# A rebuilt prologue in an attention and mixture-of-experts block: routing keys on TensorE, first row maxima beside the low halves

## The reference

```python
xn = layernorm(x)                                # x: 32 x 256 tokens x 128, eps 1e-5
q = xn @ Wq.T                                    # 8 heads of 32
kv = xn @ Wkv_down.T                             # rank 64
k, v = kv @ Wk_up.T, kv @ Wv_up.T
attn = softmax(q @ k.T * 32 ** -0.5)             # per batch of 256 tokens and head
a = (attn @ v) @ Wo.T
keys = xn @ wr + br
expert = mod(floor(keys), 8)
for e in range(8):                               # each token keeps its own expert's y
    y = relu(xn @ W1[e] + b1[e]) @ W2[e] + b2[e] # 128 -> 512 -> 128
out = x + a + y
```

## Time and profile before

| | |
|---|---|
| median of three runs | 561.96 us |
| the profiled execution | 561.93 us, of which the span shown is 560.1 us |
| busy share of the span | TensorE 83%, VectorE 84%, ScalarE 68%, GpSimd 70% |
| prologue (to the first exponential) | about 101 us |
| a unit in the first half | about 10.4 us |

### The profile page before, as it was taken

One profiled execution on the slowest core, in us unless ns is written; L12 is line 12 of the kernel. 1 busy time (PEld: TensorE's weight loads), 2 busy tenths in 40 slices (PEclk: granted clock), 3 DMA queues, 4 the chain that ended last, 5 costly groups with the idle time before them and its releaser, 6 DMA issues.

```text
span 560.1 us, 15849 instructions
## 1 busy us (share of the span) xinstructions
PE 462.7 (83%) x5016; PEld 299.0 (53%) x5016; DVE 471.7 (84%) x1000; ACT 382.0 (68%) x957; POOL 392.3 (70%) x362
## 2 busy tenths in 40 slices
PE   0433444999999999998699999998989999999984
PEld 0222211545455455455499999996545545645532
DVE  4897749799999999989688888887698988988985
ACT  0767931576777777777577777775677867877784
POOL 4166740689889888944377777775977977978970
PEclk9999757899999999999999999999999999999998
DMA  7995363455456456444778888881544764755531
GB/s 187 291 380 200 143 156 76 91 131 122 109 120 133 108 116 134 106 86 103 232 215 272 266 260 265 272 254 50 133 100 104 146 127 112 146 120 117 106 82 49
DMA packets 84956, 87.08 MB, mean 155 GB/s; under 512 B 10433, under 2 KB 66337, under 8 KB 84897
## 3 DMA queue, kind: packets, MB, share of 16 engines
q1 hardware_dynamic: 80800, 77.92, 53.1%
q0 software_dynamic: 4096, 8.40, 6.6%
HBM read 38.94 MB, written 22.04 MB: 109 GB/s over the span
## 4 chain that ended last, share of the span: by engine, by line
PE 38%; DVE 18%; issue 17%; POOL 14%; DMA 4%; SPq 4%; ACT 3%; DVEq 1%; POOLq 1%; ACTq 0%
POOL split L444 12%; PE psum L1061 8%; PE psum L1091 8%; DVE negm L858 6%; PE psum L1075 6%; PE psum L1106 4%; PE psum L1012 3%; PE psum L1124 3%; PE psum L1013 3%; PE psum L1014 3%; DVE oTl L872 2%; DMA stk<-mT 2%; DVE split L757 2%; DVE acc L877 2%; SPq L286 1%
## 5 line engine op out<-in xcount | busy, mean ns | idle before, releaser
L598 ACT ACTIVATE prob<-psum 128x512 f32<-128x512 f32 x256 | 151.1, 593 | 94.4 <-PE psum L1075 93.3
L858 DVE TENSOR_REDUCE negm<-psum 128x2 f16<-128x512 f32 x256 | 172.8, 683 | 36.6 <-PE psum L1061 35.3
L490 POOL TENSOR_TENSOR padd<-prob 128x512 f32<-128x512 f32 x120 | 139.2, 1160 | 44.9 <-ACT prob L598 42.8
L1061 PE MATMUL psum<-stk 96*128 96x256 f16 x512 | 100.7, 279 | 12.4 <-DVE negm L858 11.3
L444 POOL TENSOR_TENSOR split<-xTl,split 128x512 f16<-128x512 f32 x72 | 83.3, 1157 | 33.1 <-DVE split L948 33.1
L667 ACT ACTIVATE xTl<-psum,xn_all 128x128 f32<-128x128 f32 x288 | 82.0, 368 | 28.2 <-POOL split L444 23.4
L1075 PE MATMUL psum<-stk 97*128 97x256 f16 x512 | 98.0, 273 | 3.3 <-DMA stk<-mT 2.9
L460 POOL DMA_INDIRECT xsort<-xn_all,pos x64 | 63.0, 984 | 31.2 <-DVE pos L840 19.1
L1061 PEld LDWEIGHTS psum<-stk 96*128 96x128 f16 x512 | 38.2, 99 | 72.0 <-DVE negm L858 33.4
L468 POOL DMA_INDIRECT xn_all<-ysort,pos x64 | 64.1, 1001 | 12.1 <-issue 8.9
L1091 PE MATMUL psum<-prob,vt 128*32 128x256 f32 x1024 | 68.5, 385 | 0.7 <-ACT prob L598 0.7
(11 more groups left out here) (143 smaller groups left out, 984.7 us busy)
## 6 DMA issues: line engine op xcount, KB each, us to landing
stk<-split SPq DMA_DIRECT2D x192, 128.0 KB
xn_all<-wsplit SPq DMA_DIRECT2D x72, 258.0 KB, 4.3
xsort<-prob SPq DMA_DIRECT2D x9, 512.0 KB, 6.4
xTh<-xsort SPq DMA_DIRECT2D x18, 256.0 KB, 3.9
ysort<-xTh SPq DMA_DIRECT2D x18, 256.0 KB, 4.1
stk<-W SPq DMA_DIRECT2D x16, 256.0 KB, 5.5
wsplit<-stk SPq DMA_DIRECT2D x16, 256.0 KB, 3.8
out<-acc SPq DMA_DIRECT2D x16, 256.0 KB
```

The lines of the kernel that those rows point to most:

```text
L490: nc.gpsimd.tensor_tensor(padd[:, bb, hs], prob[:, bb, hs, 0, :], prob[:, bb, hs, 1, :], ALU.add).then_inc(pool_add, 1)
L598: nc.scalar.activation(prob[:, bb, h, :, :].rearrange("p a c -> p (a c)"), bank[2 + n % 2], ACT.Exp, scale=SCALE).then_inc(act_exp, 1)
L858: V.tensor_reduce(negm[:, k % 2, col:col + 2], bank[n % 2].rearrange("p (a c) -> p a c", a=2), AX.X, ALU.max, negate=True).then_inc(dve_ma ...
L1061: ins = mm(bank[n % 2][:, qc * T:(qc + 1) * T], stk[0:96, s, 1, h, t0 + qc * P:t0 + (qc + 1) * P], stk[0:96, s, 0, h, t0:t0 + T], start=Tr ...
```

## The change

Tokens are laid out in `acc` in another order inside a batch: partition p holds tokens 2p and 2p + 1, for the loads of x and for the stores of the output. The first quarter of x comes in four transfers, each with its own semaphore, and the other three quarters behind the small weights. ScalarE no longer waits for the small weights ahead of the first square root.

The prologue's loop is one step after the other on all engines. ScalarE normalises two chunks of a step and GpSimd the other two. TensorE makes the routing keys from `xTh` and `xTl` against `wr` in three float16 parts (eight small products for a step, `token_keys`). The projections for units 0 to 2, the values of unit 0, and unit 0's scores and row maxima lie between the steps. An expert's weights are split after the steps of the table `WSTEP` = (4, 6, 8, 9, 11, 12, 14, 15). The ranks are cut in four parts, made by VectorE in rounds 0, 2, 4 and 6 of unit 0. The eight stores of zeros, now from one row of zeros, are issued in units 0 and 1, around the loads for later units. The scatters run in units 2 to 14, and the loads of the experts' second matrices (`load_w2`) are shifted by that. Statistics, constants and staging have other homes in SBUF.

The cut diff:

```diff
+            for s in range(4):
+                sp.dma_start(acc_of(4 * s, 4), rows_of(x_rows, 4 * s, 4)).then_inc(sp_x0[s], 16)
...
+            for q in range(1, 4):
+                sp.dma_start(acc_of(q * NC // 4, NC // 4), rows_of(x_rows, q * NC // 4, NC // 4)).then_inc(sp_x[q], 16)
+
+            def load_weights(e):
+                sp.dma_start(wstage[e % 4][:, 0:F], W1[e]).then_inc(sp_w[e % 4], 16)
+                sp.dma_start(wstage[e % 4][:, F:2 * F].rearrange("p (c d) -> p c d", c=FC),
+                             W2[e].rearrange("(c p) d -> p c d", p=P)).then_inc(sp_w[e % 4], 16)
 
             def store_weights(e):
+                sp.wait_ge(pool_lo, e + 1)
...
+                    zeros = half == 0 and first and k < 2
+                    if zeros:
+                        store_zeros(4 * k)
+                        store_zeros(4 * k + 1)
                     if not (last and k >= 1):
                         load_stack(u + 3, k + 3)
+                    if zeros:
+                        store_zeros(4 * k + 2)
                     if not (last and k == 3):
                         load_max(u + 1, k + 1)
+                    if zeros:
+                        store_zeros(4 * k + 3)
                     if stores:
...
+                load_w2(E - 2, 0, NIT // 2)
                 load_w2(E - 1, 1, NIT // 2)
...
+            for e in range(4):
+                load_weights(e)
+            load_stack(0, 0)
+            load_stack(1, 1)
+            sp.wait_ge(act_cast, 3)
+            sp.dma_start(wsplit[:, :, F:W1E // 2].rearrange("e p c -> p e c"),
+                         b1c[:].rearrange("p (e c) -> p e c", e=E)).then_inc(sp_b1, 16)
+            for e in range(E):
+                if e == 6:
+                    sp.wait_ge(pool_const, 8)
+                    for j in range(2):
+                        sp.dma_start(stk[96:97, j, 0, :, :], ones16[4 * j:4 * j + 4, :]).then_inc(sp_ones[0], 16)
+                    load_max(0, 0)
                 store_weights(e)
+                if e < 4:
+                    load_weights(e + 4)
...
+            pool.wait_ge(sp_small, 16 * 10)
+            step(nc.gpsimd.tensor_copy(wr_i, wr_f))
+            step(nc.gpsimd.tensor_copy(wr_c, wr_i))
...
+            def norm(s):
+                pool.wait_ge(dve_ln, s // 4 + 1)
+                for ch in (4 * s + 2, 4 * s + 3):
+                    ins = nc.gpsimd.tensor_scalar(xn_all[:, ch, :], acc[:, ch, :], lnb[:, 3, ch:ch + 1],
+                                                  lnb[:, 4, ch:ch + 1], ALU.mult, ALU.add)
+                ins.then_inc(pool_xn, 1)
+
+            def weights_low(e):
+                pool.wait_ge(act_w, e + 1)
+                nc.gpsimd.tensor_tensor(
+                    wblk[:, e % 2, :, 1, :], wstage[e % 4].rearrange("p (b n) -> p b n", b=8),
+                    wblk[:, e % 2, :, 0, :], ALU.subtract).then_inc(pool_lo, 1)
+
+            for s in range(NSB):
+                norm(s)
+                if s in WSTEP:
+                    weights_low(WSTEP.index(s))
+            for e in range(len(WSTEP), E):
+                weights_low(e)
...
+            root(0)
+            for s in range(NSB):
+                act.wait_ge(dve_ln, s // 4 + 1)
+                norm(s)
+                if s == 0:
+                    act.wait_ge(sp_small, 16 * 10)
+                    act.wait_ge(dve_set, 1)
+                    cast(wq_s[:, 0, :], wq_f, WS)
+                    cast(wo_s[:, 0, :, :].rearrange("p g d -> p (g d)"), wo_f, WS)
+                    cast(b1c[:], b1c[:], WS)
+                    cast(b2s[0:E, :], b2_f[0:E, :], WS)
+                    cast(b2s[32:32 + E, :], b2_f[32:32 + E, :], WS)
+                    act.wait_ge(pe_fold, 1)
+                    cast(wk_s[:, 0, :], bank[6][:, 0:256], WS)
+                    cast(wv_s[:, 0, :], bank[6][:, 256:512], WS)
+                evac(s)
+                if s == 1:
+                    k_high(0, 0)
+                    q_high(0, 0)
+                if s == 2:
+                    k_high(1, 1)
+                    q_high(1, 1)
+                if s == 4:
+                    v_copy(0, 0)
+                    k_high(2, 2)
+                if s == 5:
+                    q_high(2, 2)
+                if s == 13:
+                    max_T(0, 7)
+                if s % 4 == 1 and s < 12:
+                    root(s // 4 + 1)
+                if s in WSTEP:
+                    expert_weights(WSTEP.index(s))
+            nc.scalar.preload_act_table_set("natural_log_exp_and_others")
+            act.wait_ge(pool_lo, E)
             body(0, True, False)
...
+                dve.wait_ge(pool_const, 12)
+                dve.wait_ge(pe_key, NSB)
+                step(V.reduce_sum(keys, bank[5][:, 0:6 * NC].rearrange("p (c s) -> p c s", s=6), AX.X))
+                step(V.tensor_scalar(keys, keys, 1.0 / WS, br_f, ALU.mult, ALU.add))
+                step(V.tensor_copy(ki, keys))
...
+            def ranks(part):
+
+                if part == 0:
+                    dve.wait_ge(pe_rank, 1)
+                    dve.wait_ge(dve_rt, 1)
+                    V.tensor_tensor_scan(cum.rearrange("p e c -> p (e c)"), place,
+                                         bank[4], 0.0, ALU.mult, ALU.add).then_inc(dve_rank, 1)
+                    dve.wait_ge(dve_rank, 1)
+
...
+                        if f and half == 0 and n in (0, 2, 4, 6):
+                            ranks(n // 2)
...
+            for s in range(4):
+                statistics(s)
+            variance(0)
+            statistics(4)
+            scale_bias(0)
+            for s in range(5, 8):
+                statistics(s)
+            variance(1)
+            weight_lows()
+            for s in range(NSB):
+                low_T(s)
+                if s == 1:
+                    k_low(0, 0)
+                    q_low(0, 0)
+                if s == 2:
+                    k_low(1, 1)
+                    q_low(1, 1)
+                if s == 4:
+                    k_low(2, 2)
+                if s == 5:
+                    q_low(2, 2)
+                if 4 <= s < 12:
+                    row_max(0, s - 4, 0)
+                if s < 8:
+                    statistics(8 + s)
+                if s in (3, 7):
+                    variance(s // 4 + 2)
+                if s in (0, 4, 8):
+                    scale_bias(s // 4 + 1)
+            expert_ids()
             for n in range(LEAD - 8):
                 row_max(1, n, 1)
             body(0, 0, True, False)
...
+                pe.wait_ge(dve_xTl, s + 1)
+                for c in range(4 * s, 4 * s + 4):
+                    toks = slice(c * P, (c + 1) * P)
+                    mm(bank[5][:, 6 * c:6 * c + 3], xTh[:, toks], wr_s[:, 0:3], start=True, stop=True)
+                    ins = mm(bank[5][:, 6 * c + 3:6 * c + 6], xTl[:, toks], wr_s[:, 0:3], start=True, stop=True)
+                ins.then_inc(pe_key, 1)
...
+                        if not (f and half == 0 and n < 2):
+                            scores_T(u, n, k)
+                        if f and half == 0 and n == 2:
+                            pe.wait_ge(dve_rank, 1)
+                        if n == 1 and half == 0 and first and k == 1:
+                            pe.wait_ge(dve_rank, 2)
...
+            for s in range(NSB):
+                token_T(s)
+                if s >= 1:
+                    if s == 1:
+                        pe.wait_ge(dve_ws, 5)
+                        pe.wait_ge(pool_const, 19)
+                    token_keys(s - 1)
...
+                if 4 <= s < 12:
+                    scores(0, s - 4, 0, 0)
+                if s == 12:
+                    pe.wait_ge(dve_kl, 3)
+                    transpose_max(0, 0, 7)
+            token_keys(NSB - 1)
+            for n in range(2):
+                scores(1, n, 1, 0)
+            pe.wait_ge(sp_ones[0], 32)
+            for n in range(2):
+                scores_T(0, n, 0)
             pe.wait_ge(dve_rt, 1)
             ohf = oh.rearrange("p e c -> p (e c)")
-            mm(bank[2], earlier, ohf, start=True, stop=True)
-            mm(bank[3], ones[:], ohf, start=True, stop=True).then_inc(pe_rank, 1)
-            for n in range(8):
```

More of the change, by code:

```diff
@@ new lines, in attention_moe_block @@
+        wr_i, wr_c, wr_d = prob_f[:, 2180:2181].bitcast(I32), prob_f[:, 2181:2182], prob_f[:, 2182:2183]
+        b2_f = prob_f[:, 2432:2432 + D]
+        stats = padd_f[:, 0:NC * 6].rearrange("p (c s) -> p c s", s=6)
+        lnb = padd_f[:, 384:384 + NC * 6].rearrange("p (s c) -> p s c", c=NC)
+        ones16 = padd_f[0:16, 768:768 + SB // 2].bitcast(F16)
+        keys, kf, kgt, ef = (padd_f[:, 1024 + 64 * i:1088 + 64 * i] for i in range(4))
+        ki = padd_f[:, 1280:1344].bitcast(I32)
+        iota_ti = padd_f[:, 1472:1560].bitcast(I32)
@@ L114, in attention_moe_block @@
+        earlier = padd_f[:, 1736:1864]
         oTh_f = oTh[:, :, :, :].rearrange("p a b c -> p (a b c)").bitcast(F32)
```

(23 more changed lines are left out.)

350 lines of the change are left out of this document (126 added, 224 removed).

## The result

The changed kernel takes 583.8 us (median of four runs, 583.41 to 584.09), the kernel before beside it 561.88 (561.4 to 564.86): a ratio of **1.0383, interval 1.0359 to 1.0406**, 3.8% slower. The forecast was 580.0 with a range of 567 to 594. The profiled execution has a span of 581.3 us, 21.2 above that of before; the mean granted clock is 0.92.

A forecast was written before the change was run, and what follows sets the result against it. The prologue was taken as bound by DMA, then ScalarE, then a tail with no engine full; after the change, by each step's chain. +12.6 to the sixth row maximum, +5 ranks, +0.7 load: +18.3 on 561.93, 580 us, range 567 to 594.

The forecast's parts named there:

- The loop's chain: Prologue loop: each step one chain, 4.5 us behind a split instead of 2.45; last xTh at 100.1 us, 29.7 later.
- The tail: Last xTh to unit 1's sixth row maximum: ends at 113.3 us, +12.6; expert numbers priced at 4.2.
- The ranks: VectorE in unit 0: 6.5 us of ranks only partly fit, some held by GpSimd's adds; +5, bounds 3 and 8.
- The zeros: Stores in units 0 and 1: nothing, but barely; rival: they hold the next units, +14, 594 us, chance 0.12.
- The scatters' move: Scatters two units later, onto a GpSimd with the same load in each: nothing.
- The second matrix: One more load ahead of the experts' first loads: 0 to 1.5 us, taken +0.7.
- The pairing: Loads of x and stores of the output: longer DMA packets, off the path, nothing.
- The clock: TensorE in the prologue: rival that the clock rises with fewer gaps, 15 us less, 565 us, chance 0.1.
- The -15 for all of the loop: Prologue: transposes, projections, keys and counting products all at the faster clock, 15 us less.
- The keys' share: Routing keys on TensorE in the loop: 0.9 us for eight products; with projections 6 us of the faster clock's gain.

The follow-up runs named there:

- Experiments 1 and 2: 1: changed kernel, GpSimd normalises step s + 1 ahead of the split behind step s, 566.99 us; 2: also ScalarE normalises it ahead of writing xTh, 556.36 us.
- kernels 8 and 9: 8: changed kernel, constant sel made before the loop, 580.06 us; 9: that plus GpSimd's and ScalarE's normalising ahead and zeros stored in the prologue, ratio 0.9823.
- experiment 6: Changed kernel with the four parts of the ranks together ahead of unit 0 instead of in its rounds: 585.74 us.
- experiment 4: Changed kernel with the eight stores of zeros issued in the prologue instead of in units 0 and 1: 580.01 us.
- experiment 5: Kernel before the change with only the pairing of tokens in loads of x and stores of the output: 557.55 us, ratio 0.9932.
- experiment 10: Changed kernel without the pairing of tokens, all else kept: ratio 1.0403.
- experiment 7: Changed kernel with dummy products on TensorE from step 6 on and ahead of the counting products: 577.98 us.

## Why the prediction was right, step by step

**The loop's chain: right, and shown.** Behind a split 4.89 us instead of 4.5, plain 2.57 instead of 2.45; GpSimd's chunk took 0.44 us, inside the bounds from the earlier trace rows (0.29 to 0.80) and above the 0.33 taken. By the cycles per element of the Trainium skill (GPSIMD Engine Reference, Elementwise) a chunk is an estimated 0.2 us plus dispatch; the measured 0.44 would leave 0.24 for that. The last `xTh` ended at 97.8 against a forecast of 100.1. Two errors set off each other. Up to the start of step 6 (46.5 against 51.1) the loop was 4.6 us shorter than forecast: it began at 15.4 and not at 17.0, since the second quarter came sooner, and the eight key products take 0.25 us, not 0.9 (their starts lie 0.03 apart). From there to the end of the last `xTh` it was 2.3 us longer (51.3 against 49.0), which is what six steps behind a split make at 0.39 more each. Experiments 1 and 2 give back 27.4 us, more than the whole loss of 21.9.

**The tail: its sum by luck.** +13.3 against +12.6: the loop's end came 2.3 us sooner than forecast, and the expert numbers cost 7.4 us and not 4.2. The 4.4 us from which they were priced contain one hold themselves. GpSimd's last subtraction of the kernel before covers their first instruction, the 1.30 of L807 in the earlier trace rows (0.26 in kernels 8 and 9), and the casts behind it ran while GpSimd stood still:

```profile
74.11 2.13 POOL L437 TENSOR_TENSOR stk<-stk 128x1024 f16<-128x1024 f32 x1
```

The hold of the earlier trace rows was known, and I charged it to the ranks alone. Kernels 8 and 9 show it: 7.4, 5.0, 3.2 us as GpSimd's work goes away.

**The ranks: right in size.** +5.9 between the sixth row maximum and unit 2's maxima, against +5 with bounds 3 and 8. Moved out of unit 0, in experiment 6, they leave it at 10.0 us from maxima to maxima instead of 14.2. Two of the ranks instructions were held, to 1.23 and 1.79 us.

**The zeros: taken at nothing, cost 2.5 to 3 us.** The stretch from 128 to 140 us has the DMA share at 1.09 and 268 GB/s, below the 304 of the earlier trace rows that I reckoned with. The "nothing, but barely" was just not enough. The scatters' move was taken at nothing too: without zeros units 1 and 2 are 1.1 us shorter each than before (experiment 4), probably by the scatters that are gone from them, and most of the zeros' cost is hidden behind that. The Trainium skill (DMA: Bandwidth & Descriptors, Specifications) gives 512 bytes as enough for line rate; experiment 5, with 353 GB/s for pieces of 1024 bytes and 304 for 512 on the same queue at a full share, does not agree, nor does experiment 10 (357 against 291, with weights among the loads).

**The second matrix: +0.7 forecast, not measured.** The lag behind the kernel before is 20.8 us at the last unit of the half, 20.4 at the experts' first product and 21.2 at the end. The first product's wait differs by up to 3 us between traces of nearly the same kernel, so no run here tells what the load costs.

**The pairing: "off the path, nothing" is nearly right for the changed kernel and wrong for the kernel before.** Without pairs the changed kernel is 0.7 us later at the loop's end, and its time does not differ clear of noise (1.0403 against 1.0383). In the kernel before, where DMA is full from 16.5 to 50 us in the earlier trace rows, pairs give 4 us. So the loop's chain took away what the pairing alone would have won, and the forecast counted it on neither side.

**The clock.** The price of a step was right: 0.5 us for four transposes forecast, 0.46 measured in steps 7 to 15 of experiment 7, and 5.8 us with the counting products. The -15 for all of the loop was never put to the test, since steps 1 to 5 with their projections had no dummies. Steps 2 and 3, which happened to run at the upper level in kernel 4, were 1.35 us shorter together. The keys' share in it is nothing: eight key products take 0.25 us at either level.

## What to carry to other kernels

When a loop is cut into steps that pass through several engines, write the next step's first operation ahead of this step's long side work on *every* engine: one call moved on GpSimd was worth 17 us here, one on ScalarE 10 more. Price small VectorE operations by what GpSimd does at that moment, not by their own row in another stretch. And where a stretch is full of DMA, treat the length of a contiguous piece as a cost of its own.

## Not expected of the hardware

- A VectorE cast of 128x64 takes 0.20 us alone, 2.00 beside a GpSimd subtraction of 128x1024, with which it ends, and 2.88 where a memset follows that at once; two others take 1.0 beside two selects.
- Products of 128x128 weights by 3 columns start 0.03 us apart, weight loads included, at either level of the clock.
- With the DMA engines fully busy, loads in pieces of 1024 bytes ran at 353 GB/s where pieces of 512 ran at 304.
- The row of the granted clock read 1.00 over 50 us in one trace in which transposes took the 430 ns that they take where it reads 0.50.
- Dummy products raised the granted clock from 0.50 to 0.97 and helped a kernel with gaps of 3 to 4 us on TensorE by 5.8 us; the same dummies cost 1.1% where the loop was pipelined.
